# First attention's output: the few rows with an inner term computed apart, the RMS weight folded into Wo

## The chip, the cores and the metric

One program runs on one core of a Trainium2 chip. The metric is device time in microseconds: the median of three runs of the kernel before is 3495.94 (3495.18 to 3498.05). The program is a whole decoder of four layers (self attention, cross attention and a feed-forward part in each); the change touches only the last stage of the first self attention, some 63 us of it.

## The reference

The first self attention of the decoder works on B = 2 batches of 1024 tokens, 4 heads of 64, in chunks of 64 tokens. After the chunks' `W` and `U` are made, a scan over the chunks carries a state `S`; only its diagonal `Sd` is used for the output:

```python
def chunk_step(S, inp):
    q_i, k_i, w_i, u0 = inp
    Sd = jnp.diagonal(S, axis1=-2, axis2=-1)
    u_i = u0 - w_i * Sd[:, None]
    o_inter = q_i * Sd[:, None]
    A_i = jnp.tril(jnp.einsum('bchd,bchd->bc', q_i, k_i))
    o_intra = A_i[:, :, None, None] * u_i
    S = S + jnp.einsum('bchd,bche->bhde', k_i, u_i)
    return (S, o_inter + o_intra)
...
o = o * jax.lax.rsqrt(jnp.mean(o * o, axis=-1, keepdims=True) + EPS) * g
out = o.reshape(Bx, Lx, NH * HD) @ Wo
```

`A_i` is a table of batches by rows of the chunk, [2, 64], and `tril` keeps of it only row 0 of batch 0 and rows 0 and 1 of batch 1. So the inner term `A_i * u_i` is zero except in the first one or two rows of each chunk; everywhere else the output is `q_i * Sd`. `g` has one weight per place in a head (64 of them) and is the same for every head and token.

## The kernel before

The 2048 tokens lie in `NT` = 16 tiles of 128 tokens, and each tile holds two chunks of 64 (partitions 0 to 63 and 64 to 127). `QK` (trace name `q_k_tokens`) holds q and k of a token side by side, `KV` (`beta_k_v`) holds w and u by then. Work is written out in phases; inside a phase each engine has its own list of instructions and waits on semaphores, and at the end of a phase all engines meet. There is no planner: the order is the order of the code.

Three phases matter here. In the **scan phase** VectorE scans the chunk sums into `diag`, the diagonal of the state before each of the 32 chunks (32 x 256), while GpSimd builds `sel`, a 32 x 2048 table that is 1 where a token belongs to a chunk, and `rowm`, the mask of first rows. Then comes `arrive`, in which SyncE waits until all late loads have landed. Then the **output phase**:

- TensorE (L3197) multiplies `sel` by `diag` for each tile: this spreads the chunk's diagonal over its 128 tokens, into one of four PSUM banks. One such float32 product is two MATMUL records in the trace.
- VectorE does for each tile (L3213 to L3220): the dot product of q and k, w times d, the dot times the mask, u minus that, q times d, and dot times u plus q times d into `O`. There are three drains per tile, each of which lets the pipeline run empty.
- ScalarE squares each tile of `O` (L3244) into one of two buffers, VectorE sums per head (L3224), and when all 16 are summed one square root (L3246) and one reciprocal (L3226) follow.
- VectorE multiplies each tile by the reciprocal (L3230), GpSimd multiplies it by `g` (L3236), TensorE turns it (L3203, two transposes), and ScalarE copies it to `OT` (L3249).

Last, `finish` multiplies by `Wo` (L162), adds the residual and does the layer norm; its own order is not touched.

## Time and profile before

| what | us |
|---|---|
| median of three runs | 3495.94 |
| profiled execution, its own time | 3497.36 |
| span of its trace | 3495.6 |
| scan phase begins | 243.6 |
| output phase, first product to last copy | 248.75 to 311.64 |
| of this: products (16 tiles on VectorE) | 250.0 to 287.7 |
| of this: squares and sums | 287.8 to 295.3 |
| of this: scaling, weight, turning and copying | 296.3 to 311.6 |
| next phase (`finish`) begins | 311.9 |

Times within the trace count from its start. Busy time of an engine is read beside its idle time: an engine that is nearly always busy in a stretch sets its length. "Granted clock" is TensorE's, as a share of 2.4 GHz, so 0.50 is the 1.2 GHz level.

### The profile page before, as it was taken

What the parts mean: (1) busy time and instruction counts of PE and PEld (TensorE: products, weight loads), DVE (VectorE), ACT (ScalarE), POOL (GpSimd) and SP (SyncE); (2) the same over time, 40 slices, a digit from 0 to 9 for tenths busy, and PEclk for the clock granted to TensorE, in tenths of its full rate; (3) what the DMA queues carried; (4) which work ended last, traced back from release to release, by engine and by line L of the source; (5) the groups of instructions that cost most, each with busy time, mean ns of one, the idle gap of its engine ahead of it and who ended that gap; (6) DMA issues with size and microseconds to landing.
All of it is one profiled execution on the core that took longest, in us unless ns stands there. A gap on an engine that the chain in (4) does not pass through costs nothing. (4 is left out here: it accounts for less than half of the span.)

```text
span 3495.6 us, 54010 instructions
## 1 busy us (share of the span) xinstructions
PE 2866.3 (82%) x18533; PEld 1739.5 (50%) x18565; DVE 1939.8 (55%) x4670; ACT 1564.7 (45%) x4333; POOL 712.8 (20%) x790
## 2 busy tenths in 40 slices
PE   6586994845999998679968998989988968959993
PEld 3443562332555555345634653446533445639993
DVE  6546674343878876576726662156522647842333
ACT  4313782322777776572224562135521228813331
POOL 3201010021211220012104560045500102301113
PEclk9686996868999999889978999999999989959996
DMA  1000002010000000000001001000000000051112
GB/s 68 1 2 14 1 2 79 0 55 12 1 1 2 1 2 24 37 13 1 17 0 38 1 1 59 0 6 1 1 27 12 7 21 2 2 223 32 36 36 80
DMA packets 34789, 80.46 MB, mean 23 GB/s; under 512 B 8577, under 2 KB 23570, under 8 KB 30450
## 3 DMA queue, kind: packets, MB, share of 16 engines
q1 hardware_dynamic: 29746, 64.61, 5.1%
q0 software_dynamic: 4368, 11.93, 1.2%
q8 instruction: 137, 2.24, 0.3%
q14 instruction: 106, 0.87, 0.1%
q10 hardware_dynamic: 432, 0.80, 0.1%
HBM read 63.31 MB, written 14.02 MB: 22 GB/s over the span
## 5 line engine op out<-in xcount | busy, mean ns | idle before, releaser
L2436 ACT ACTIVATE scores<-scores,min 128x128 f32<-128x128 f32 (+7 forms) x256 | 198.5, 775 | 86.1 <-DVE min L2419 82.1
L2417 DVE TENSOR_SCALAR zero_marks<-psum 128x128 f32<-128x128 f32 (+7 forms) x256 | 192.0, 750 | 66.6 <-PE psum L2349 64.8
L2419 DVE CUSTOM_DVE_ANT_0 scores<-psum,zero_marks 128x128 f32<-128x128 f32 (+7 forms) x256 | 193.9, 758 | 29.9 <-issue 0.9
L2356 PE MATMUL psum<-ident,scores 128*128 128x128 f32 x1152 | 172.8, 277 | 16.4 <-ACT probsT L2453 13.3
L2453 ACT ACTIVATE probsT<-psum 128x128 f32<-128x128 f32 (+7 forms) x256 | 163.0, 637 | 31.7 <-PE psum L2356 31.1
L3684 PE MATMUL psum<-Hn,W 128*128 128x512 f32 x384 | 170.1, 606 | 8.2 <-PEq L415 8.2
L1574 ACT ACTIVATE XT<-psum,b_of_tile 128x128 f32<-128x128 f32 x312 | 89.0, 368 | 177.5 <-PE psum L1494 177.5
L1494 PE MATMUL psum<-x_gatheredT,XT 128*128 128x128 f32 x1248 | 152.0, 281 | 6.0 <-issue 3.1
L1494 PEld LDWEIGHTS psum<-x_gatheredT,XT 128*128 128x128 f32 x1248 | 147.1, 196 | 12.9 <-issue 11.8
L2356 PEld LDWEIGHTS psum<-ident,scores 128*128 128x128 f32 x1152 | 123.2, 141 | 55.8 <-issue 29.8
L2346 PE MATMUL psum<-XT,Q_heads 64*128 64x512 f32 x256 | 143.7, 641 | 0.0
L3542 POOL TENSOR_TENSOR probs<-probs,stat 128x512 f32<-128x512 f32 (+1 forms) x128 | 123.2, 986 | 99.8 <-DVE stat L3506 97.3
L1503 PE MATMUL psum<-W,XT 128*128 x624 | 141.2, 379 | 0.6 <-DVE y L1548 0.6
L3556 ACT ACTIVATE probs<-psum,stat 128x256 f32<-128x256 f32 (+1 forms) x256 | 114.4, 460 | 47.1 <-DVE stat L3499 47.1
L3410 POOL TENSOR_TENSOR straight<-straight,crossed 128x512 f32<-128x512 f32 x64 | 81.1, 1268 | 224.6 <-DVE crossed L3400 224.6
L3684 PEld LDWEIGHTS psum<-Hn,W 128*128 128x128 f32 x384 | 74.7, 195 | 103.7 <-issue 103.7
L1503 PEld LDWEIGHTS psum<-W,XT 128*128 128x128 f32 x624 | 115.5, 190 | 15.1 <-issue 1.0
L3700 DVE SCALAR_TENSOR_TENSOR GT<-psum,b,gelu 128x512 f32<-128x512 f32 x48 | 36.0, 751 | 142.0 <-ACT gelu L3694 142.0
L3499 DVE TENSOR_REDUCE stat<-psum 128x2 f32<-128x512 f32 (+1 forms) x128 | 78.1, 652 | 50.7 <-PE psum L3450 22.2
L848 ACT ACTIVATE probs<-probs,stat 128x154 f32<-128x154 f32 x256 | 104.9, 412 | 2.7 <-DVE stat L786 2.7
L2347 PE MATMUL psum<-XT,Q_heads_turned 64*128 64x128 f32 (+3 forms) x256 | 102.8, 482 | 0.0
L2340 PE MATMUL psum<-XT,Q_heads 128*128 128x128 f32 (+3 forms) x256 | 96.2, 458 | 3.3 <-POOL Q_heads L2318 2.8
(619 smaller groups left out, 6860.8 us busy)
## 6 DMA issues: line engine op xcount, KB each, us to landing
W<-in_L3f_W SPq DMA_DIRECT2D x16, 1024.0 KB, 22.5
L3f_y_rows<-y SPq DMA_DIRECT2D x39, 128.0 KB, 1.7
L0f_rows<-Xtok SPq DMA_DIRECT2D x2, 2048.0 KB, 7.7
W<-in_L0f_W SPq DMA_DIRECT2D x3, 1152.0 KB
early_weights<-in_L2f_Wqkv SPq DMA_DIRECT2D x2, 1536.0 KB
W<-in_L2f_W SPq DMA_DIRECT2D x2, 1536.0 KB
XT<-in_xT SPq DMA_DIRECT2D x1, 2048.0 KB, 10.3
Xtok<-in_xtok SPq DMA_DIRECT2D x1, 2048.0 KB
```

What stands on the lines that cost most here:

```text
L848: last = act.activation(p, src, ACT.Exp, bias=st(n, 0)[:, h:h + 1], scale=-1.0, accum_out=st(n, 1)[:, h:h + 1])
L1494: ins = pe.matmul(K.bank[2 * q + part][:, m * P:(m + 1) * P], W1t[:, k * INTER + (part * HALF + m) * P:k * INTER + (part * HALF + m + 1) * P],
L1503: ins = pe.matmul(K.bank[6][:, 0:D], HT[:, q, c, :], W2[:, bass.ds(at + c * D, D)], start=(c == 0), stop=(c == IC - 1))
L2346: pe.matmul(sc(i)[:, 0:BLK], Qh[own, u % 2, h, :], KT[own, c, b * S:b * S + BLK], start=True, stop=True, skip_group_check=True)
L2356: ins = pe.transpose(turned[:, kt * P:(kt + 1) * P], Sc[:, i % ROT, kt * P:(kt + 1) * P], K.ident[:])
L2417: dve.tensor_scalar(zero[:, i % 2, 0:n], sc(i)[:, 0:n], 0.0, -NEG, ALU.is_equal, ALU.mult)
L2419: dve.tensor_tensor_reduce(Sc[:, i % ROT, 0:n], sc(i)[:, 0:n], zero[:, i % 2, 0:n], 1.0, -NEG, ALU.add, ALU.min, low[:, i % ROT:i % ROT + ...
L2436: act.activation(p, p, ACT.Exp, bias=low[:, i % ROT:i % ROT + 1], scale=-1.0, accum_out=sums[:, u % 2, h:h + 1]).then_inc(s["exp_done"], 1)
L2453: act.activation(PT[:, i % SLOTS, 0:n], turned[:, 0:n], ACT.Copy).then_inc(s["pt_out"], 1)
L3542: pool.tensor_tensor(v, v, inner(stat[:, t % 2, 2, 2 * g:2 * g + 2], ks.stop - ks.start), ALU.mult).then_inc(s["normed"], 1)
L3556: act.activation(Pr[:, t % 2, h, ks], K.bank[2 * G + hh][:, c0 + ks.start:c0 + ks.stop], ACT.Exp, bias=stat[:, t % 2, 0, h:h + 1], scale=- ...
L3684: ins = pe.matmul(K.bank[2 * (n % 4) + part][:], W1[:, k, (part * HC + m) * P:(part * HC + m + 1) * P], Hn[:, k, j * BLK:(j + 1) * BLK], s ...
```

## The change

The output phase no longer makes the inner term for all tokens. Its parts:

- In the scan phase eight transfers between places of SBUF (four issued by SyncE for q and k, four by ScalarE for w and u) gather rows 0 and 1 of every chunk into compact tiles of 64 partitions: partition 32 i + c holds row i of chunk c. GpSimd makes `rowc`, a column of ones with zeros for row 1 of batch 0, in place of `rowm`.
- TensorE makes the diagonal for the compact rows first, in two products with 32 result rows each.
- VectorE makes the whole six-step computation once on these 64 rows, with its semaphore waits in place of drains; for each of the 16 tiles it then makes only q times d.
- SyncE writes the compact result back over rows 0 and 1 of the chunks in `O`: four transfers after the products of batch 0, four after those of batch 1. ScalarE's squares of each batch wait for them.
- Squares, sums, root, reciprocal, scaling and turning go in four groups of four tiles, with one group's squares ahead of the last group's scaling. There are four buffers of squares (two before) and two PSUM banks for the turned tiles (four before).
- `g` is loaded as one column of 128 and multiplied into `Wo` by one ScalarE instruction at the start of the phase; GpSimd has no work left in the output phase.

```diff
@@ -2795,7 +2795,7 @@
...
 Wo = sbuf(es, nc, "Wo", [P, DC, D])
 OT = sbuf(es, nc, "OT", [P, DC, TOK])
-g4 = sbuf(es, nc, "g", [P, D])
+gc = sbuf(es, nc, "g", [P, 1])
...
@@ -2819,7 +2819,7 @@
             @block.sync
             def _(sp):
-                sp.dma_start(g4[:], spread(w["L0a_g"])).then_inc(K.late, 16)
+                sp.dma_start(gc[:], w["L0a_g"][0:P].rearrange("(p o) -> p o", o=1)).then_inc(K.late, 16)
                 sp.dma_start(Wo[:], w["L0a_Wo"]).then_inc(K.late, 16)
             @block.gpsimd
@@ -3145,8 +3145,26 @@
     diag = sbuf(q_life, nc, "diagonal", [NCH, D])
     sel = sbuf(q_life, nc, "chunk_select", [NCH, TOK])
-    rowm = sbuf(q_life, nc, "first_rows", [P, B])
+    CR = 2 * P // CH * NT
+    C4 = 2 * NT
+    rowc = sbuf(q_life, nc, "row_within_batch", [CR, 1])
+    qk_c, wu_c = (sbuf(q_life, nc, n, [CR, 2 * D]) for n in ("first_rows_q_k", "first_rows_w_u"))
+    PER = NT // B
+    first_rows = lambda v, i, half, t: v[half * CH + i:half * CH + i + 1, t, :]
+    of_rows = lambda v, i, half, t: v[i * C4 + 2 * t.start + half:i * C4 + 2 * t.stop:2, :]
+    rows_of = [(i, half) for i in range(B) for half in range(2)]
+    K.late_count += 16 * 2 * len(rows_of)
     with ExitStack() as inn, phase(nc, K.sems, "step scanned turned") as (block, s):
+        @block.sync
+        def _(sp):
+            for i, half in rows_of:
+                sp.dma_start(of_rows(qk_c, i, half, slice(0, NT)), first_rows(QK, i, half, slice(0, NT))).then_inc(K.late, 16)
+        @block.scalar
+        def _(act):
+            for i, half in rows_of:
+                act.dma_start(of_rows(wu_c, i, half, slice(0, NT)), first_rows(KV, i, half, slice(0, NT))).then_inc(K.late, 16)
...
@@ -3154,12 +3172,11 @@
         def _(pool):
             v = sel[:].rearrange("p (n j) -> p n j", j=CH)
             pool.memset(sel[:], 1.0).then_inc(s["step"], 1)
-            pool.memset(rowm[:], 1.0).then_inc(s["step"], 1)
+            pool.memset(rowc[:], 1.0).then_inc(s["step"], 1)
             pool.wait_ge(s["step"], 2)
             pool.affine_select(out=v, in_=v, compare_op=ALU.is_equal, fill=0.0, base=0, pattern=[[-1, NCH], [0, CH]], channel_multiplier=1)
-            pool.affine_select(out=rowm[0:CH], in_=rowm[0:CH], compare_op=ALU.is_ge, fill=0.0, base=0, pattern=[[1, B]], channel_multiplier=-1)
-            pool.affine_select(out=rowm[CH:P], in_=rowm[CH:P], compare_op=ALU.is_ge, fill=0.0, base=0, pattern=[[1, B]], channel_multiplier=-1)
+            pool.memset(rowc[C4:C4 + 2 * PER], 0.0)
         @block.vector
         def _(dve):
@@ -3182,71 +3199,114 @@
     arrive(nc, K)
-    with ExitStack() as inn, phase(nc, K.sems, "d_done o_done squared summed root scaled o_normed turned out") as (block, s):
-        tmp = sbuf(inn, nc, "tmp", [P, 2, D])
-        dot = sbuf(inn, nc, "dot", [P, NT])
-        sq = sbuf(inn, nc, "squares", [P, 2, D])
+    with ExitStack() as inn, phase(nc, K.sems, "d_done rows_d_done dot_done dot_cut wd_done u_done qd_done rows_done rows_in0 rows_in1 o_done squared summed root recip scaled turned out") as (block, s):
+        rows_in = (s["rows_in0"], s["rows_in1"])
+        wd, u_c, qd, o_c = (sbuf(inn, nc, n, [CR, D]) for n in ("rows_w_d", "rows_u", "rows_q_d", "rows_o"))
+        dot = sbuf(inn, nc, "dot", [CR, 1])
+        sq = sbuf(inn, nc, "squares", [P, 4, D])
         ms = sbuf(inn, nc, "mean_square", [P, NT, L0H])
         O = sbuf(inn, nc, "O", [P, NT, D])
+        GRP = 4
+        groups = [range(a, a + GRP) for a in range(0, NT, GRP)]
+        @block.sync
+        def _(sp):
+            sp.wait_ge(s["rows_done"], 1)
+            for b in range(B):
+                sp.wait_ge(s["o_done"], (b + 1) * PER)
+                own = slice(b * PER, (b + 1) * PER)
+                for i, half in rows_of:
+                    sp.dma_start(first_rows(O, i, half, own), of_rows(o_c, i, half, own)).then_inc(rows_in[b], 16)
         @block.tensor
         def _(pe):
+            cut = sel[:, 0:TOK:CH]
+            for i in range(B):
+                ins = pe.matmul(K.bank[6][i * C4:(i + 1) * C4, 0:D], cut, diag[:], start=True, stop=True, skip_group_check=True)
+            ins.then_inc(s["rows_d_done"], 1)
             for t in range(NT):
                 if t >= 4:
                     pe.wait_ge(s["o_done"], t - 3)
                 pe.matmul(K.bank[t % 4][:, 0:D], sel[:, t * P:(t + 1) * P], diag[:], start=True, stop=True).then_inc(s["d_done"], 1)
             for t in range(NT):
-                pe.wait_ge(s["o_normed"], t + 1)
-                if t >= 4:
-                    pe.wait_ge(s["out"], t - 3)
+                pe.wait_ge(s["scaled"], t + 1)
+                if t >= 2:
+                    pe.wait_ge(s["out"], t - 1)
                 for c in range(DC):
-                    ins = pe.transpose(K.bank[4 + t % 4][:, c * P:(c + 1) * P], O[:, t, c * P:(c + 1) * P], K.ident[:])
+                    ins = pe.transpose(K.bank[4 + t % 2][:, c * P:(c + 1) * P], O[:, t, c * P:(c + 1) * P], K.ident[:])
                 ins.then_inc(s["turned"], 1)
         @block.vector
         def _(dve):
-            for t in range(NT):
-                q_, k_ = QK[:, t, 0:D], QK[:, t, D:2 * D]
-                a, b_ = tmp[:, 0, :], tmp[:, 1, :]
+            def product(t):
                 dve.wait_ge(s["d_done"], t + 1)
-                d_ = K.bank[t % 4][:, 0:D]
-                dve.tensor_tensor_reduce(a, q_, k_, 1.0, 0.0, ALU.mult, ALU.add, dot[:, t:t + 1])
-                dve.tensor_tensor(b_, KV[:, t, 0:D], d_, ALU.mult)
-                dve.drain()
-                dve.tensor_tensor(dot[:, t:t + 1], dot[:, t:t + 1], rowm[:, t // 8:t // 8 + 1], ALU.mult)
-                dve.tensor_tensor(b_, KV[:, t, D:2 * D], b_, ALU.subtract)
-                dve.tensor_tensor(a, q_, d_, ALU.mult)
-                dve.drain()
-                dve.scalar_tensor_tensor(out=O[:, t, :], in0=b_, scalar=dot[:, t:t + 1], in1=a, op0=ALU.mult, op1=ALU.add).then_inc(s["o_done"], 1)
-                dve.drain()
-            for t in range(NT):
-                dve.wait_ge(s["squared"], t + 1)
-                dve.reduce_sum(ms[:, t, :], sq[:, t % 2, :].rearrange("p (h d) -> p h d", h=L0H), AX).then_inc(s["summed"], 1)
-            dve.wait_ge(s["root"], 1)
-            dve.reciprocal(ms[:], ms[:])
-            dve.drain()
-            for t in range(NT):
-                v = O[:, t, :].rearrange("p (h d) -> p h d", h=L0H)
-                dve.tensor_tensor(v, v, inner(ms[:, t, :], D // L0H), ALU.mult).then_inc(s["scaled"], 1)
-        @block.gpsimd
-        def _(pool):
-            for t in range(NT):
-                pool.wait_ge(s["scaled"], t + 1)
-                pool.tensor_tensor(O[:, t, :], O[:, t, :], g4[:], ALU.mult).then_inc(s["o_normed"], 1)
+                dve.tensor_tensor(O[:, t, :], QK[:, t, 0:D], K.bank[t % 4][:, 0:D], ALU.mult).then_inc(s["o_done"], 1)
+            def sums_of(g):
+                for t in groups[g]:
+                    dve.wait_ge(s["squared"], t + 1)
+                    dve.reduce_sum(ms[:, t, :], sq[:, t % 4, :].rearrange("p (h d) -> p h d", h=L0H), AX).then_inc(s["summed"], 1)
+            def scale(g):
+                a = groups[g]
+                dve.wait_ge(s["root"], g + 1)
+                dve.reciprocal(ms[:, a.start:a.stop, :], ms[:, a.start:a.stop, :]).then_inc(s["recip"], 1)
+                dve.wait_ge(s["recip"], g + 1)
+                for t in a:
+                    v = O[:, t, :].rearrange("p (h d) -> p h d", h=L0H)
+                    dve.tensor_tensor(v, v, inner(ms[:, t, :], D // L0H), ALU.mult).then_inc(s["scaled"], 1)
+            d_c = K.bank[6][0:CR, 0:D]
+            dve.tensor_tensor_reduce(u_c[:], qk_c[:, 0:D], qk_c[:, D:2 * D], 1.0, 0.0, ALU.mult, ALU.add, dot[:]).then_inc(s["dot_done"], 1)
+            dve.wait_ge(s["rows_d_done"], 1)
+            dve.tensor_tensor(wd[:], wu_c[:, 0:D], d_c, ALU.mult).then_inc(s["wd_done"], 1)
+            dve.tensor_tensor(qd[:], qk_c[:, 0:D], d_c, ALU.mult).then_inc(s["qd_done"], 1)
+            dve.wait_ge(s["dot_done"], 1)
+            dve.tensor_tensor(dot[:], dot[:], rowc[:], ALU.mult).then_inc(s["dot_cut"], 1)
+            dve.wait_ge(s["wd_done"], 1)
+            dve.tensor_tensor(u_c[:], wu_c[:, D:2 * D], wd[:], ALU.subtract).then_inc(s["u_done"], 1)
+            product(0)
+            dve.wait_ge(s["dot_cut"], 1)
+            dve.wait_ge(s["qd_done"], 1)
+            dve.wait_ge(s["u_done"], 1)
+            dve.scalar_tensor_tensor(out=o_c[:], in0=u_c[:], scalar=dot[:], in1=qd[:], op0=ALU.mult, op1=ALU.add).then_inc(s["rows_done"], 1)
+            for t in range(1, NT):
+                product(t)
+            sums_of(0)
+            for g in range(len(groups)):
+                if g + 1 < len(groups):
+                    sums_of(g + 1)
+                scale(g)
         @block.scalar
         def _(act):
-            for t in range(NT):
-                act.wait_ge(s["o_done"], t + 1)
-                if t >= 2:
-                    act.wait_ge(s["summed"], t - 1)
-                act.activation(sq[:, t % 2, :], O[:, t, :], ACT.Square).then_inc(s["squared"], 1)
-            act.wait_ge(s["summed"], NT)
-            act.activation(ms[:], ms[:], ACT.Sqrt, scale=1.0 / (D // L0H), bias=K.eps[:, 0:1]).then_inc(s["root"], 1)
-            for t in range(NT):
-                act.wait_ge(s["turned"], t + 1)
-                act.activation(OT[:, :, t * P:(t + 1) * P], K.bank[4 + t % 4][:, 0:D].rearrange("p (c k) -> p c k", c=2), ACT.Copy).then_inc(s["out"], 1)
+            def squares(g):
+                for t in groups[g]:
+                    if t % PER == 0:
+                        act.wait_ge(rows_in[t // PER], 16 * len(rows_of))
+                    if t >= 4:
+                        act.wait_ge(s["summed"], t - 3)
+                    act.activation(sq[:, t % 4, :], O[:, t, :], ACT.Square).then_inc(s["squared"], 1)
+            def root(g):
+                a = groups[g]
+                act.wait_ge(s["summed"], a.stop)
+                act.activation(ms[:, a.start:a.stop, :], ms[:, a.start:a.stop, :], ACT.Sqrt, scale=1.0 / (D // L0H), bias=K.eps[:, 0:1]).then_inc(s["root"], 1)
+            def turned_out(g):
+                for t in groups[g]:
+                    act.wait_ge(s["turned"], t + 1)
+                    act.activation(OT[:, :, t * P:(t + 1) * P], K.bank[4 + t % 2][:, 0:D].rearrange("p (c k) -> p c k", c=2), ACT.Copy).then_inc(s["out"], 1)
+            act.activation(Wo[:].rearrange("p c n -> p (c n)"), Wo[:].rearrange("p c n -> p (c n)"), ACT.Copy, scale=gc[:, 0:1])
+            squares(0)
+            for g in range(len(groups)):
+                if g + 1 < len(groups):
+                    squares(g + 1)
+                root(g)
+                if g >= 1:
+                    turned_out(g - 1)
+            turned_out(len(groups) - 1)
 finish(nc, K, lambda k, t: Wo[:, k, :], tile_of_block(OT), DC)```

On VectorE, in the output phase, before the change (`tmp` and `first_rows` are scratch and mask; this piece comes 16 times, then 16 sums and 16 scalings):

```order
L3213 ISA tmp,dot<-q_k_tokens 128x256
L3213 ISA dot 128x1
L3214 TENSOR_TENSOR tmp<-beta_k_v,psum 128x256
L3216 TENSOR_TENSOR dot<-dot,first_rows 128x1
L3217 TENSOR_TENSOR tmp<-beta_k_v,tmp 128x256
L3218 TENSOR_TENSOR tmp<-q_k_tokens,psum 128x256
L3220 SCALAR_TENSOR_TENSOR O<-tmp,dot 128x256
```

And what stands there on VectorE after the change (`rows_...` are the compact tiles):

```order
L3265 TENSOR_TENSOR dot<-dot,row_within_batch 64x1
L3267 TENSOR_TENSOR rows_u<-first_rows_w_u,rows_w_d 64x256
L3243 TENSOR_TENSOR O<-q_k_tokens,psum 128x256
L3272 SCALAR_TENSOR_TENSOR rows_o<-rows_u,dot,rows_q_d 64x256
L3243 TENSOR_TENSOR O<-q_k_tokens,psum 128x256 x15
L3248 TENSOR_REDUCE mean_square<-squares 128x4 x8
L3253 RECIPROCAL mean_square<-mean_square 128x16
L3257 TENSOR_TENSOR O<-O,mean_square 128x256 x4
```

One instruction per tile is left of seven, and sums and scalings now alternate in groups of four.

On ScalarE, in the scan and output phases, the difference (`Wo<-Wo,g` is the folded weight):

```order
-L3238 UNCONDITIONAL_BRANCH
-L3244 ACTIVATE squares<-O 128x256 x16
-L3246 ACTIVATE mean_square<-mean_square,eps 128x64
-L3249 ACTIVATE OT<-psum 128x2x128 x16
+L3166 DMA first_rows_w_u<-beta_k_v 16x1x512 x4
+L3301 ACTIVATE Wo<-Wo,g 128x512
+L3289 ACTIVATE squares<-O 128x256 x8
+L3294 ACTIVATE mean_square<-mean_square,eps 128x16
+L3289 ACTIVATE squares<-O 128x256 x4
+L3294 ACTIVATE mean_square<-mean_square,eps 128x16
+L3299 ACTIVATE OT<-psum 128x2x128 x4
```

The copies of a group now stand behind the squares of the group after the next, in one queue on ScalarE.

## Rows read from the trace of the kernel before

**Rows 1.** Windows: length; busy PE, PEld, DVE, ACT, POOL (starts); clock; transfers' share, GB/s.
```profile
260.00:270.00 10.00, 5.43 (x10) 1.98 (x8) 8.80 (x31) 0.00 (x0) 0.00 (x0) 0.50 0.00 0
300.00:308.00 8.00, 6.36 (x19) 2.61 (x18) 8.00 (x10) 3.47 (x10) 8.00 (x10) 0.50 0.00 0
```

**Rows 2.** Timeline, scan phase's GpSimd work: start, length, engine, line, [idle <- releaser].
```profile
243.63 1.79 POOL L3156 MEMSET chunk_select<- 32x2048 f32 x1 [34.05 <-POOLq L54]
247.89 0.18 POOL L3162 TENSOR_SCALAR_AFFINE_SELECT first_rows<-first_rows 64x2 f32<-64x2 f32 x1
248.75 3.05 PEld L3197 LDWEIGHTS psum<-diagonal,chunk_select 32*128 32x128 f32 x8 [3.10 <-issue]
```

**Rows 3.** Timeline, one tile's products on VectorE, and the last one.
```profile
250.00 0.42 DVE L3213 CUSTOM_DVE_ANT_0 tmp<-q_k_tokens 128x256 f32<-128x256 f32 x1 [3.62 <-PE psum L3197]
...
256.01 0.41 DVE L3218 TENSOR_TENSOR tmp<-q_k_tokens,psum 128x256 f32<-128x256 f32 x1
...
257.11 0.43 DVE L3213 CUSTOM_DVE_ANT_0 tmp<-q_k_tokens 128x256 f32<-128x256 f32 x1
...
287.25 0.48 DVE L3220 SCALAR_TENSOR_TENSOR O<-tmp,dot 128x256 f32<-128x256 f32 x1
```

**Rows 4.** Timeline, from the squares to the start of the next phase.
```profile
289.75 0.75 DVE L3224 TENSOR_REDUCE mean_square<-squares 128x4 f32<-128x256 f32 x2 [0.22 <-ACT squares L3244]
295.34 0.35 ACT L3246 ACTIVATE mean_square<-mean_square,eps 128x64 f32<-128x64 f32 x1 [0.49 <-DVE mean_square L3224]
296.34 12.87 DVE L3230 TENSOR_TENSOR O<-O,mean_square 128x256 f32<-128x256 f32 x16
309.86 1.37 PE L3203 MATMUL psum<-ident,O 128*128 128x128 f32 x4 [0.18 <-POOL O L3236]
311.26 0.38 ACT L3249 ACTIVATE OT<-psum 128x256 f32<-128x256 f32 x1 [0.30 <-PE psum L3203]
311.93 7.31 PEld L162 LDWEIGHTS psum<-Wo,OT 128*128 128x128 f32 x28 [1.10 <-issue]
```

**Rows 5.** Timeline of an earlier phase, and L3230's row (durations min/median/max).
```profile
127.27 11.89 POOL L2970 TENSOR_TENSOR q_k_tokens<-q_k_tokens,norms 128x256 f32<-128x256 f32 x16 [4.36 <-DVEq L2953]
127.28 12.15 DVE L2957 TENSOR_TENSOR q_k_tokens<-q_k_tokens,norms 128x256 f32<-128x256 f32 x16
139.52 5.45 DVE L2960 TENSOR_TENSOR beta_k_v<-q_k_tokens,beta 128x256 f32<-128x256 f32 x16
L3230 DVE TENSOR_TENSOR O<-O,mean_square x16: 418/943/944, 296.3 to 308.3; 128x256 f32<-128x256 f32 x16
```

**Rows 6.** TensorE: lines' rows (durations, starts), windows, and one timeline row.
```profile
L3197 PE MATMUL psum<-diagonal,chunk_select x8: 626/626/759, 248.8 to 251.9; 32*128 32x256 f32 x8
L162 PE MATMUL psum<-Wo,OT x18: 379/379/379, 315.2 to 318.8; 128*128 128x256 f32 x18
...
253.00:254.00 1.00, 0.52 (x2) 0.50 0.00 0
...
336.39 9.94 PE L374 MATMUL psum<-XT,early_weights 128*128 128x512 f32 x16 [1.10 <-PEq L415]
...
314.00:315.00 1.00, 1.00 (x5) 0.79 (x4) 0.42 (x1) 0.00 (x0) 0.00 (x0) 0.60 1.10 336
...
342.00:343.00 1.00, 1.00 (x3) 0.95 0.00 0
```

**Rows 7.** An issue on SyncE's queue; issues with KB each and us to landing.
```profile
312.29 0.43 SPq L154 DMA_DIRECT2D early_weights<-in_L0x_Wk  x1
...
L3f_y_rows<-y SPq DMA_DIRECT2D x39, 128.0 KB, 1.7
L0f_rows<-acc SPq DMA_DIRECT2D x1, 512.0 KB, 2.8
Wd<-in_L1a_Wd SPq DMA_DIRECT2D x1, 128.0 KB, 2.0
b<-in_L3f_b SPq DMA_DIRECT2D x1, 32.0 KB, 25.1
```

## The prediction

> **What bounds the kernel now.** I read the windows of the output phase first, then its timeline, then the rows of single lines. In the windows VectorE is busy 8.80 of 10 us while it makes the products, TensorE works half the time at clock 0.50, and GpSimd does nothing; in the scaling, VectorE and GpSimd are both busy 8.00 of 8 us [rows 1]. The timeline gives the same in time. VectorE starts the first tile at 250.00 and the fourth at 257.11, so one tile takes (257.11 - 250.00) / 3 = 2.37 us, and the last ends at 287.25 + 0.48 = 287.73 [rows 3]. ScalarE squares the first two tiles early and then waits for VectorE, so 14 of 16 squares lie in the stretch behind the products, 287.8 to 295.3, at about 0.48 us a tile. The root starts at 295.34, the scaling of 16 tiles takes 12.87 us from 296.34, and turning and copying follow it with the last copy ending at 311.26 + 0.38 = 311.64; the next phase starts its weights at 311.93 [rows 4]. No other phase runs beside this one, since all engines meet at its ends. Whatever the output phase and the entry to it lose, the kernel loses, one for one.
>
> **The entry.** GpSimd sets the end of the scan phase: its work begins at 243.63 and ends at 247.89 + 0.18 = 248.07, and TensorE's first weights load at 248.75 [rows 2]. The change takes away two small mask steps (0.18 each by the row) and adds one memset shorter than either, so GpSimd ends near 247.8. In its place comes a new wait: four transfers on SyncE's queue and four on ScalarE's, at 0.43 us each to issue plus a gap to 0.47 (rows 7 has the 0.43), so the last is issued at 243.63 + 3 x 0.47 = 245.0. The trace shows no transfer from SBUF to SBUF. The nearest rows are 1.7, 2.0 and 2.8 us from issue to landing for 128, 128 and 512 KB; the rows moved here are 32 KB a transfer [rows 7]. With 2.0 they land at 247.0, before GpSimd ends; with 2.8 at 247.8, level with it. I take the start of the phase as unchanged, 248.75, with -0.3 and +1.0 as bounds.
>
> **The products.** TensorE has two more products than before, 18 in place of 16, each of two passes: 36 passes. At clock 0.50 eight passes start from 248.8 to 251.9, 0.44 us apart, and one lasts 0.63 [rows 6]. VectorE's one instruction per tile costs 0.41 (L3218, the same instruction) [rows 3], less than TensorE's 0.88 per tile, so TensorE becomes the pace: 35 x 0.44 = 15.4, to 264.15, plus 0.63 plus 0.41 gives **265.2** for the end of the products, against 287.73: 22.5 us less. The compact computation (two products for it first on TensorE, counted above; seven instructions on VectorE, each no longer than 0.48, 2.4 us in all with hand-overs of about 0.1 added to some) is hidden: it starts when the compact diagonal is there, near 250.8, delays tile 0's product to about 252.5, and TensorE first needs a bank back for tile 4 at 248.75 + 12 x 0.44 = 254.0. Without that cover it would cost its 2.4 us. The two compact products write different partitions; if they run beside each other the sum is 0.9 lower.
>
> **The rows written back.** SyncE's first four transfers are issued when tile 7 is done, eight tiles or 7 us ahead of the end of the products, and have landed by 265.2 - 7.0 + 3 x 0.47 + 2.0 = 261.6: hidden. The four for batch 1 start at 265.2 and land at 265.2 + 0.1 + 1.4 + 2.0 = **268.7**. Queued behind this wait on ScalarE are the squares of groups 2 and 3, the roots 1 to 3, and every copy to `OT`. VectorE is not idle meanwhile: it sums groups 0 and 1 (8 tiles at 0.36, from 0.75 for two [rows 4]) until 268.2 and scales group 0 from 268.5.
>
> **The scaling.** In place of 12.87 us for 16 tiles [rows 4] I take 5.45. The evidence is in this trace: 16 multiplies of 128x256 by a spread-out column take 12.15 us beside GpSimd's own 11.89 us of the same work, and the 16 that follow with GpSimd idle take 5.45; and L3230 itself has a minimum of 418 ns against a median of 943, its first instance starting before GpSimd has anything to do [rows 5]. GpSimd's weight step is gone, so four tiles cost 1.4.
>
> The Trainium skill (SBUF — State Buffer, section SBUF: two separate sides) says that VectorE, with two inputs from SBUF, and GpSimd hold a port pair exclusively, one blocking the other for a whole instruction. The trace agrees, by 5.45 against 12.15 us; the rule would give the same sum.
>
> **The tail.** From 268.7 ScalarE's queue is the pace, since VectorE's share for two groups of sums and three of scaling is 2 x 1.5 + 3 x 1.4 plus reciprocals, under 9. ScalarE: squares of group 2 1.4 (two take 0.75, [rows 4] by their sums), root 0.3, four copies, squares of group 3 1.4, root 0.3, four copies, root 0.3, eight copies. A copy is 0.38, and four transposes take 1.37 [rows 4]; with two banks one bank's round is 0.69 + 0.38 + 0.1 of hand-over = 1.17 for two tiles, which makes about 2.0 for a group whose first two tiles wait already. Sum: 2 x 1.4 + 3 x 0.3 + 4 x 2.0 = 11.7, so the last copy ends at **280.4**. The weight's fold costs one ScalarE instruction of 128x512 at the start of the phase, when ScalarE waits for the first rows until 261.6: hidden. Its price uncovered would be under 0.8, twice a 128x256 copy.
>
> **The sum.** 311.64 - 280.4 = 31.2 us less. Of it 22.5 are the products, 7.4 the faster scaling, and the rest the overlap less the 3.5 us wait for rows. Against the profiled execution's 3497.36 that is 3466.2; the median lies 1.4 below that execution, which gives **3465**. Bounds: entry -0.3 to +1.0, compact products 0 to -0.9, landings 1.7 to 2.8 in place of 2.0, -0.3 to +0.8, copies at 0.38 a tile as floor (-1.9 in all, as the first groups are covered) or 0.69 (+2.8): 3462 to 3470 with the clock at 0.50.
>
> **The rivals.**
>
> The clock rises in the products. Before, TensorE worked half the time there and never left 0.50; now it has no pause until its last tile. For it: with the products of `finish`, begun at 311.96, the clock has risen within 314 to 315, and with those begun at 336.39 just after 342, so 2.9 and 5.6 us on [rows 4, 6]. Against it: the first products here already ran without a pause from 248.75, ten starts up to 253, and at 254 the clock is still 0.50 [rows 6]; they hold 32 partitions, the others 128. If it rises at about 4.7 us, 11 passes are done and 25 go at (318.8 - 315.2) / 17 = 0.21 [rows 6], 0.42 a tile, level with VectorE's 0.41: 25 x 0.23 = 5.7 less. That gives 3459.5.
>
> The Trainium skill (TensorE: Matmul & The Clock Gate, Part 1) has the throttle released by sustained matmul activity; by it alone this rival would be the forecast. The trace agrees at 314.8 and 342 and does not at 253 to 254.
>
> The scaling stays slow, so that the change doesn't do what it says: then the 943 ns come from writing in place, not from GpSimd. For it: L2957 writes to the tile it reads and L2960 does not. Against it: L3230's first instance is in place and takes 418 [rows 5]. VectorE would be the pace: 12.87 / 16 = 0.80 a tile, scale 0 from 268.5 to 271.7, then three times sums 1.5, 0.2 and scaling 3.2, the last turned and copied 1.2 on: 287.6 at most, 285 to 286 with overlaps of successive instructions. That is 5.5 more: 3470.5.
>
> Landings are slow for single-partition transfers, say 5 us: the entry is 245.0 + 5.0 + 0.7 = 250.7, 2.0 later, and the rows come 3.0 later: 3470.
>
> Slower than before: each transfer lands like the slowest small one in the trace, `b<-in_L3f_b`, 32 KB, 25.1 us [rows 7]. Then the entry moves by 245.0 + 25.1 + 0.7 - 248.75 = 22.1 and the last squares by 23.1, in all 45.2 on 3465: 3510. It decides from about 18 us a landing. Against it: that transfer was one of a row of large loads from HBM, and here nothing else moves: the transfers' share in this stretch is 0.00 [rows 1].
>
> **Chances.** Forecast 0.52, clock rising 0.27, slow landings 0.09, slow scaling 0.07, slower 0.03, something that eats the gain whole 0.02. The likeliest gives 3465. The range reaches down past 3459.5 with the same spread below, 3457, and up over both 3470s with half of theirs, 3474. Faster than before by over 0.2% (7 us, about what a measurement of this kernel can tell from no change): 0.95; within: 0.02; slower: 0.03.
>
> **What would show it.** In the profile after: the first products' weights still at 248 to 249; TensorE without a pause for some 15 us at clock 0.50, and L3243 16 times at about 0.41; L3219's rows landing some 2 us after issue and ScalarE's first square of group 2 waiting for them; L3257 at 415 ns, not 830 or 943; the next phase's first weights at 280 to 281. Wrong would be: a clock of 1.00 within the products (gain near 36), the squares of group 2 waiting over 5 us, L3257 over 800 ns, or `finish` or a later phase longer than before by a microsecond or more.

## The result and the profile after

The changed kernel takes 3467.9 us (median of five runs, 3465.74 to 3476.39) where the kernel before takes 3495.18 beside it (five runs, 3490.76 to 3498.05). The ratio is 0.9929, with a 95% interval of 0.9917 to 0.9942: faster by about 0.7%. The forecast was 3465, in a range of 3457 to 3474.

Times of the trace count from its start, and the scan phase itself begins 1.14 us earlier than before (242.49 against 243.63 [rows 2]). The code ahead of it differs only in how `g` is loaded, and in the twelve kernels below the scan phase begins anywhere from 241.09 to 243.78, so nothing is read from this. Stages are therefore compared from the start of the scan phase, GpSimd's first memset of `chunk_select`. This is the timeline of after: start, length, engine, line, output and input; in brackets the idle time ahead of the group and what ended it.

```profile
242.48 2.94 SPq L3161 DMA_DIRECT2D first_rows_q_k<-q_k_tokens  x4
242.49 1.79 POOL L3174 MEMSET chunk_select<- 32x2048 f32 x1 [34.06 <-POOLq L54]
242.50 2.93 ACTq L3166 DMA_DIRECT2D first_rows_w_u<-beta_k_v  x4
246.59 0.09 POOL L3179 MEMSET row_within_batch<- 16x1 f32 x1
250.15 1.08 PE L3225 MATMUL psum<-diagonal,chunk_select 32*32 32x256 f32 x4 [5.36 <-PEq L415]
251.16 14.02 PE L3230 MATMUL psum<-diagonal,chunk_select 32*128 32x256 f32 x32
265.22 0.42 DVE L3243 TENSOR_TENSOR O<-q_k_tokens,psum 128x256 f32<-128x256 f32 x1 [0.43 <-PE psum L3230]
268.45 1.43 DVE L3257 TENSOR_TENSOR O<-O,mean_square 128x256 f32<-128x256 f32 x4
269.66 1.33 ACT L3289 ACTIVATE squares<-O 128x256 f32<-128x256 f32 x4 [2.06 <-DMA O<-rows_o]
279.31 0.81 ACT L3299 ACTIVATE OT<-psum 128x256 f32<-128x256 f32 x2 [0.42 <-PE psum L3236]
280.54 0.81 ACT L3299 ACTIVATE OT<-psum 128x256 f32<-128x256 f32 x2 [0.42 <-PE psum L3236]
281.63 8.12 PEld L162 LDWEIGHTS psum<-Wo,OT 128*128 128x128 f32 x28 [1.10 <-issue]
```

To be seen are four things. GpSimd is done at 246.7, yet the first product waits until 250.15. Then 36 passes follow without a pause. The last product of VectorE ends at 265.22 + 0.42 = 265.64, and ScalarE's squares of the second batch begin only at 269.66, released by a transfer. From there ScalarE works through its queue, with a pause of 0.42 at each of the last pairs of copies. Against [rows 4] the scaling of four tiles takes 1.43, not a quarter of 12.87 = 3.22.

These are single lines of after: issues and the scaling (shortest, median and longest in ns, then the first and the last start).

```profile
L3161 SPq DMA_DIRECT2D first_rows_q_k<-q_k_tokens x4: 609/684/823, 242.5 to 244.7; - x4
L3219 SPq DMA_DIRECT2D O<-rows_o x8: 634/634/770, 258.9 to 267.7; - x8
L3257 DVE TENSOR_TENSOR O<-O,mean_square x16: 415/418/425, 268.4 to 278.0; 128x256 f32<-128x256 f32 x16
```

And windows of after: stretch, length, busy time, then the granted clock, the share of the transfers and GB/s. The first is of all engines (PE, PEld, DVE, ACT, POOL), the second of TensorE alone.

```profile
244.00:246.00 2.00, 0.40 (x2) 0.11 (x2) 0.75 (x2) 0.00 (x0) 1.93 (x3) 0.80 0.97 47
...
254.00:258.00 4.00, 4.00 (x11) 0.50 0.00 0
262.00:265.00 3.00, 3.00 (x8) 0.50 0.01 3
```

TensorE is busy 4.00 of 4 us and still at clock 0.50, the 1.2 GHz level. The gathering transfers fill 0.97 of the queues' time and move 47 GB/s.

| step (us) | before | forecast | after |
|---|---|---|---|
| scan phase's start to first product | 5.15 | 5.12 | 7.66 |
| first product to end of VectorE's last | 38.95 | 16.45 | 15.49 |
| from there to the first square of tile 8 | | 3.5 | 4.02 |
| from there to the last copy's end | | 11.7 | 11.69 |
| start of scan to start of `finish` | 68.30 | 37.1 | 39.14 |

The forecast counted from the first load of weights, 0.03 ahead of the first product [rows 2].

The two phases are 68.30 - 39.14 = 29.2 us shorter; 31.2 were forecast. The whole trace is 27.8 shorter (3495.6 and 3467.8): the scan phase starts 1.14 earlier, `finish` takes 25.76 to the next phase's first product where it took 24.47 (+1.29), and all that comes later adds the other 1.2.

### The profile page after: what moved, and what is told of

Same layout as the page of the kernel before. It is cut to its first block and busy times, and to the rows that moved or that the text cites. A ratio compares the mean times of both kernels' runs of the same rounds, so it can differ in the third digit from the quotient of the medians.

```text
span 3467.8 us, 53877 instructions
## 1 busy us (share of the span) xinstructions
PE 2858.7 (82%) x18537; PEld 1737.6 (50%) x18569; DVE 1908.2 (55%) x4584; ACT 1564.9 (45%) x4337; POOL 699.3 (20%) x773
## 3 DMA queue, kind: packets, MB, share of 16 engines
HBM read 63.18 MB, written 14.02 MB: 22 GB/s over the span
## 6 DMA issues: line engine op xcount, KB each, us to landing
L3f_y_rows<-y SPq DMA_DIRECT2D x39, 128.0 KB, 1.7
```

## The experiments

Each stage length below is read from the kernel's own trace, from its scan phase's start as above. The table stands first; all columns but the first are in us, and `its length` runs from the start of `finish` to the next phase's first product. For the four kernels with one run the total is not read. Of the other edits to the changed kernel, only three_parts and all_four have a ratio to before whose interval lies clear of after's 0.9917 to 0.9942; what fold_undone, held_128 and wait_later are worth is read from stage lengths alone.

| kernel | first product | last product's end | first square of tile 8 | last copy's end | start of `finish` | its length | median (runs) |
|---|---|---|---|---|---|---|---|
| before | 5.15 | 44.10 | | 68.02 | 68.30 | 24.47 | 3495.18 (5) |
| after | 7.66 | 23.15 | 27.17 | 38.86 | 39.14 | 25.76 | 3467.9 (5) |
| fold_alone | 5.14 | 44.10 | | 59.70 | 59.98 | 23.32 | 3483.43 (6) |
| fold_undone | 7.81 | 23.30 | 27.32 | 42.48 | 42.75 | 25.39 | 3470.76 (5) |
| held_128 | 7.66 | 18.56 | 22.58 | 34.28 | 34.56 | 26.43 | 3470.24 (4) |
| wait_later | 4.90 | 20.39 | 24.40 | 36.10 | 36.38 | 25.29 | 3465.9 (4) |
| four_banks | 7.66 | 23.15 | 27.17 | 36.72 | 37.00 | 23.64 | 3463.02 (1) |
| qk_gathered_earlier | 5.12 | 20.60 | 24.62 | 36.32 | 36.59 | 25.18 | 3470.78 (1) |
| two_queues_back | 7.67 | 23.15 | 25.93 | 37.63 | 37.90 | 26.47 | 3470.89 (1) |
| no_inner_term | 4.90 | 19.35 | 21.27 | 33.72 | 33.99 | 26.50 | 3470.08 (1) |
| three_parts | 4.93 | 16.67 | 20.68 | 31.47 | 31.74 | 25.89 | 3454.66 (4) |
| all_four | 4.88 | 16.60 | 19.36 | 30.36 | 30.64 | 23.56 | 3454.61 (4) |

**fold_alone**: the kernel before with the weight's fold and nothing else.

```diff
-pool.tensor_tensor(O[:, t, :], O[:, t, :], g4[:], ALU.mult).then_inc(s["o_normed"], 1)
+act.activation(Wo[...], Wo[...], ACT.Copy, scale=gc[:, 0:1])   # first on ScalarE
-pe.wait_ge(s["o_normed"], t + 1)
+pe.wait_ge(s["scaled"], t + 1)
```

> The kernel before with one part of the change: g is loaded as a column and multiplied into Wo by ScalarE, GpSimd does nothing in the output phase. Theory (GpSimd slows VectorE): the scaling falls from 12.87 us to about 5.5, turning and copying become the pace at about 0.43 a tile, the phase ends about 7 us earlier, 3488. Rival (writing in place makes it slow): L3230's successor stays near 0.80 a tile and only GpSimd's lag goes, about 1 us, 3494.

Measured: ratio 0.9966 (0.9954 to 0.9978); the phases are 68.30 - 59.98 = 8.3 us shorter. The scaling in its timeline:

```profile
295.51 5.46 DVE L3230 TENSOR_TENSOR O<-O,mean_square 128x256 f32<-128x256 f32 x16
```

The same instruction, writing in place, takes 5.46 in place of 12.87 [rows 4] once GpSimd no longer works beside it. The rival by which writing in place was slow is dead. The phases gained a little more than the 7 expected.

**fold_undone**: the changed kernel with GpSimd's step put back between scaling and turning, and the fold gone (the diff above, reversed).

> The changed kernel with one part undone: GpSimd multiplies each tile by g between scaling and turning, Wo is left as it is. Theory: the scaling goes back from 418 ns to 830 or 943, VectorE becomes the pace behind the rows' wait, the phase is 5 to 6 us longer, 3473. Rival (ScalarE's queue is the pace anyway): the phase is under 2 us longer.

Measured: ratio to before 0.9937 (0.9924 to 0.9951), the phases 3.6 us longer than after's. That lies between the 5 to 6 of the theory and the rival's under 2. Two rows of its timeline:

```profile
272.75 2.49 DVE L3257 TENSOR_TENSOR O<-O,mean_square 128x256 f32<-128x256 f32 x4
273.25 3.26 POOL L3285 TENSOR_TENSOR O<-O,g 128x256 f32<-128x256 f32 x4 [0.73 <-DVE O L3257]
```

Four tiles cost VectorE 2.49 beside GpSimd's 3.26, against 1.43. So the fold is worth 8.3 us in the old order and 3.6 in the new one, where part of the slow scaling lies beside ScalarE's squares and copies. With GpSimd's step left as it was, the rest of the change is worth 68.30 - 42.75 = 25.5. The Trainium skill (SBUF — State Buffer, section SBUF: two separate sides) says that whichever of the two engines starts first holds their shared port pair for its whole instruction. The traces agree that each slows the other: VectorE's instruction has a median of 942 ns beside GpSimd and takes 418 without it, GpSimd's takes 902 beside VectorE and 719 without it. They do not show that one stands still for the whole of the other, since a pair of instructions comes every 0.86 us, less than 0.42 + 0.72.

**held_128**: as after, but the products hold all 128 partitions, with zeros in the new 96 rows of the diagonal. VectorE clears those rows in the scan phase, where GpSimd also makes its last memset ahead of the mask; the entry stays 7.66.

```diff
-diag = sbuf(q_life, nc, "diagonal", [NCH, D])
-sel = sbuf(q_life, nc, "chunk_select", [NCH, TOK])
+diag = sbuf(q_life, nc, "diagonal", [P, D])
+sel = sbuf(q_life, nc, "chunk_select", [P, TOK])
...
+dve.memset(diag[NCH:2 * NCH], 0.0)
+dve.memset(diag[2 * NCH:P], 0.0)
```

> The changed kernel with the spreading products holding 128 partitions in place of 32 (chunk_select and diagonal are padded with zeros; same columns, same number of passes). Theory (the clock stays at 0.50 because these products hold 32 partitions): the clock rises within 3 to 6 us of the phase's first product, the 16 products take 9 to 10 us in place of 14.0, the phase is 4 to 5 us shorter, 3463. Rival (the number of partitions doesn't matter): clock 0.50 to the last product and no change in the phase.

Measured: ratio 0.9923 (0.9905 to 0.9941). Its TensorE, the timeline and the windows around the rise:

```profile
251.44 1.09 PE L3228 MATMUL psum<-diagonal,chunk_select 128*32 128x256 f32 x4 [5.36 <-PEq L415]
252.45 9.43 PE L3233 MATMUL psum<-diagonal,chunk_select 128*128 128x256 f32 x32
...
254.00:257.00 3.00, 3.00 (x9) 0.50 0.00 0
257.00:260.00 3.00, 3.00 (x16) 0.99 0.00 0
```

The same 36 passes in the same order: held on 32 partitions, they ran their 15 us at 0.50; held on 128, the clock rose 5.6 us after the first (257.0 - 251.44) and the products ended 4.6 earlier. All of it reached the last copy (34.28 against 38.86). But the clock fell again at 267.3, `finish` had it back only 6.0 us after its start and took 26.43, and the median, 3463 by the theory, came out at 3470.24, not distinguishable from after's. The rise comes back in three_parts and all_four, 4.4 us after their first product. The Trainium skill (TensorE: Matmul & The Clock Gate, Part 1) has sustained matmul activity release the throttle; held_128 agrees, after does not, by the windows at 254 to 265 above.

**wait_later**: the gathers count on a semaphore of their own, so the phase opens without them, and VectorE makes tiles 0 to 3 before it waits for them.

```diff
-K.late_count += 16 * 2 * len(rows_of)
...
-sp.dma_start(of_rows(qk_c, ...), first_rows(QK, ...)).then_inc(K.late, 16)
+sp.dma_start(of_rows(qk_c, ...), first_rows(QK, ...)).then_inc(gathered, 16)
...
+for t in range(4):
+    product(t)
+dve.wait_ge(gathered, 16 * 2 * len(rows_of))
```

> The changed kernel with the wait for the eight gathering transfers taken out of the meeting before the output phase and put on VectorE, behind the products of tiles 0 to 3; the compact computation follows there. Theory (the entry lost 2.5 us to the transfers, the rest of the phase does not depend on them): from the scan phase's start to the first spreading product 5.1 us in place of 7.7, the whole 2.5 us shorter, 3465. Rival (the wait only moves): VectorE waits over 1 us for the rows behind tile 3 and the phase ends within 0.5 us of the changed kernel's.

Measured: ratio 0.9918 (0.9903 to 0.9934). TensorE, and one transfer row (KB each, median us from issue to landing):

```profile
248.40 1.08 PE L3226 MATMUL psum<-diagonal,chunk_select 32*32 32x256 f32 x4 [2.60 <-PEq L415]
...
first_rows_q_k<-q_k_tokens SPq DMA_DIRECT2D x4, 32.0 KB, 4.4
```

The first product comes 4.90 after the scan phase's start, 2.76 earlier than after's, and the gain stays whole to the last copy (38.86 - 36.10 = 2.76). So the entry's loss was the wait for the gathers and nothing else. A gather of q and k takes 4.4 us to land by the median, 3.4 to 5.0 in all, where 2.0 was taken.

**qk_gathered_earlier**: the four gathers of q and k are issued in the phase before, with the same wait as after.

```diff
-sp.dma_start(of_rows(qk_c, ...), first_rows(QK, ...)).then_inc(K.late, 16)   # in the scan phase
+sp.dma_start(of_rows(qk_c, ...), first_rows(QK, ...)).then_inc(K.late, 16)   # one phase ahead
```

> The changed kernel with the four gathering transfers of q and k issued one phase earlier (where the w and u products are made), so that only the four of w and u are left in the scan phase. Theory (the 128 packets of 2 KB were slow, up to 1.09 us each, because they all read from the same few partitions at once): the packets of each four take about half as long, the four of w and u land by about 247, GpSimd's mask sets the entry again, and scan start to first product is 5.1 to 5.6 us in place of 7.7. Rival (a fixed latency of such a transfer): packets as long as before, and the entry still over 7 us.

Measured: the first product at 5.12, as early as before the change, with half of the gathers still waited for. The windows with these four in flight:

```profile
244.00:246.00 2.00, 0.39 (x2) 0.11 (x2) 1.03 (x2) 0.00 (x0) 1.93 (x3) 0.88 0.68 48
246.00:248.00 2.00, 0.12 (x2) 0.15 (x4) 0.07 (x1) 0.14 (x1) 0.93 (x2) 0.50 0.24 17
```

With four gathers in flight the rate is 48 GB/s, with eight it was 47. The four are issued 0.63 us apart, and 32 KB every 0.63 us is 52 GB/s, so they ran near the pace of their issues. The eight came from two engines at about twice that pace and got no more: 256 KB took from 243.76 to 249.25. Packets of 2 KB took up to 0.67 us with four (0.45 in the mean) and up to 1.09 with eight (0.50), so the theory's half holds for the longest and not for the mean. Each gather reads one partition (0, 1, 64 or 65). That these few partitions are what held the eight to 47 GB/s is not shown: a gather spread over many partitions wasn't run.

**four_banks**: four PSUM banks for the turned tiles, as in the kernel before.

```diff
-if t >= 2:
-    pe.wait_ge(s["out"], t - 1)
+if t >= 4:
+    pe.wait_ge(s["out"], t - 3)
-ins = pe.transpose(K.bank[4 + t % 2][...], ...)
+ins = pe.transpose(K.bank[4 + t % 4][...], ...)
```

> The changed kernel with four PSUM banks for the turned tiles in place of two. Theory (with two banks a tile's transposes wait for the copy of the tile two before, so the last eight copies go at 0.61 us each): they go at under 0.5 us each and the phase ends 1 to 1.5 us earlier, 38.9 us after the scan phase's start becoming under 38. Rival (ScalarE's own queue of squares, roots and copies is the pace): under 0.3 us.

Measured: the last copy 2.14 us earlier, more than the 1 to 1.5 expected. ScalarE's last eight copies are one group now, where they came in pairs 1.23 us apart (279.31 and 280.54 above):

```profile
274.44 3.37 ACT L3299 ACTIVATE OT<-psum 128x256 f32<-128x256 f32 x8 [0.85 <-PE psum L3236]
```

**two_queues_back**: of the eight transfers that write rows back, GpSimd's queue issues half.

```diff
-for i, half in rows_of:
-    sp.dma_start(first_rows(O, ...), of_rows(o_c, ...)).then_inc(rows_in[b], 16)
+rows_back(sp, rows_of[0::2], rows_in)
+rows_back(pool, rows_of[1::2], rows_in_too)
```

> The changed kernel with the four write-back transfers of each batch issued by two engines, SyncE and GpSimd, two each. Theory (3 of the 4.0 us between the last product and the square of tile 8 are four issues of 0.68 us in a row): the wait falls to about 2.7 us and the phase is 1 to 1.3 us shorter. Rival (GpSimd's transfers start later than SyncE's, about 1 us by their queue): no gain, or up to 1 us longer.

Measured: from the last product's end to the square of tile 8 it takes 2.78, not 4.02, and the phases lose the same 1.24. ScalarE's row:

```profile
269.18 1.34 ACT L3297 ACTIVATE squares<-O 128x256 f32<-128x256 f32 x4 [0.82 <-DMA O<-rows_o]
```

**no_inner_term** leaves out the gathers, the compact rows and their write-back, so its rows 0 and 1 lack the inner term.

```diff
-ins = pe.matmul(K.bank[6][i * C4:(i + 1) * C4, 0:D], cut, diag[:], ...)
-dve.tensor_tensor_reduce(u_c[:], qk_c[:, 0:D], qk_c[:, D:2 * D], ...)      # and the five steps behind it
-act.wait_ge(rows_in[t // PER], 16 * len(rows_of))
+act.wait_ge(s["o_done"], t + 1)
```

> The changed kernel without the inner term: no gathering, no compact computation, no write-back, the squares wait for each product alone (the first rows' inner term is left out of the output). It shows what the few rows cost in all. Theory (2.5 us at the entry, 1.0 for TensorE's two compact products, and about 3 of the 4.0 before the squares of tile 8, since squares that run beside the products shorten the tail too): scan and output phases 31 to 33 us in place of 39.1. Rival (VectorE's sums, scaling and ScalarE's queue behind the products are the pace, not the rows' return): 35 us or more.

Measured: the phases take 33.99 us, 5.15 less than after's, so the gain is smaller than the theory's 31 to 33 would have it. The entry gives 2.76 and the compact products 1.04 (15.49 to 14.45). The wait falls by 2.1 (4.02 to 1.92), but the tail behind it is 0.76 longer (12.45). VectorE begins its sums only behind its last product, and ScalarE's squares of tiles 4 to 7 wait for them; the first copies then wait 0.57 us at 265.42 for tiles that VectorE has scaled late, while after's, at 271.10, find them ready:

```profile
261.83 1.39 ACT L3250 ACTIVATE squares<-O 128x256 f32<-128x256 f32 x4 [10.22 <-DVE mean_square L3224]
```

This is what the inner term costs now: 5.15 of 39.14 us.

**three_parts** is wait_later, held_128 and four_banks together; **all_four** has the two queues for the write-back as well. Their edits are the diffs above.

> The changed kernel with three edits together: the wait for the gathered rows behind tile 3's product, the spreading products holding 128 partitions, and four PSUM banks for the turned tiles. If the single gains add (2.8 and 4.6 us measured, 1 to 1.5 expected), the scan and output phases take 30 to 31 us in place of 39.1 and the whole about 8 us less than the changed kernel, 3460. Rival (the clock then falls or the rows come back too late): the compact rows are not ready for the write-back of batch 0, or the wait before the squares of tile 8 grows, and the gain is under 6 us.

> The three edits together (31.7 us for the two phases) and the write-back split over SyncE and GpSimd, which alone took 1.24 us off. Theory: 30.5 us, the whole about 1 us below the three edits, 3453 to 3454; against the changed kernel about 14 us less. Rival (the wait is covered by something else by now): two phases within 0.3 us of 31.7.

Measured: three_parts has a ratio of 0.9887 (0.987 to 0.9903), all_four 0.9886 (0.9869 to 0.9902). Singly the three parts gave 2.76 + 4.58 + 2.14 = 9.5 us, together 39.14 - 31.74 = 7.4. The timelines show the two places where the other 2.1 went. The first, in all_four, is the same in three_parts:

```profile
253.96 3.72 PE L3241 MATMUL psum<-diagonal,chunk_select 128*128 128x256 f32 x16 [1.15 <-DVE O L3254]
```

With the faster clock TensorE runs out of banks while VectorE is in the compact computation: 1.15 us of idle time, where after has none. wait_later, with the same order at clock 0.50, has none either, so the cover that the forecast named for this computation is lost where the clock has risen by then. From the first product to VectorE's last, three_parts takes 11.74 us and held_128 10.90, 0.84 less.

The second place, in three_parts, is behind the products, which end at 258.57:

```profile
259.58 2.56 ACT L3295 ACTIVATE squares<-O 128x256 f32<-128x256 f32 x8 [12.05 <-DMA O<-rows_o]
260.02 2.70 DVE L3252 TENSOR_REDUCE mean_square<-squares 128x4 f32<-128x256 f32 x8 [1.46 <-ACT squares L3295]
```

The rows of batch 0 now come back behind the last product, where in after they were home by 263.05, ahead of its end at 265.64. So the squares of tiles 0 to 7 and VectorE's sums start a microsecond late, and the tail behind the first square of tile 8 takes 10.79 us against 9.55 in four_banks, the other 1.24. The rival on record with three_parts looked near here: it had the compact rows not ready for this write-back. They were ready, SyncE issues it at 255.41, but from there to the first square it takes 4.2 us, which the shorter products no longer cover.

all_four is 1.1 us shorter than three_parts in the phases and 2.3 in `finish`, yet equal in the median (3454.61 and 3454.66), so this difference lies below what the totals tell. Both beat the changed kernel, by 13.2 and 13.3 us in the median.

## Why the prediction was right, and the step that was mis-sized

- **Direction and size: right.** The phases lost 29.2 us of the 31.2 forecast, and the products gave most of it, as said. The scaling's share is smaller than the 7.4 named for it: with everything else in place it is worth 3.6 (fold_undone).
- **The entry: mis-sized.** "I take the start of the phase as unchanged, 248.75, with -0.3 and +1.0 as bounds" failed: it came 2.5 later (7.66 against 5.15), outside the bounds. Two inputs were wrong. A gather's issue took 0.61 to 0.82 us on SyncE, not the 0.43 of [rows 7], so the last stood 2.2 us behind the scan's start and not 1.4. And it landed 4.4 us after issue by the median and 5.0 at most (read in wait_later), not 2.0. The slow-landings rival had priced about that at the entry (5 us a landing, 2.0 later), but put the same delay on the rows written back, and those did not have it. wait_later and qk_gathered_earlier each took the delay away alone.
- **The products: right.** TensorE was the pace at clock 0.50, 0.44 a pass (32 passes in 14.02), VectorE waited 0.43 for each tile. They took 15.49, not 16.45: the two compact products ran beside each other, four passes in 1.08 us, which was the -0.9 given as a bound.
- **The clock rival: did not happen here**, though it did in held_128, at 5.6 us. The stated evidence against it, 32 partitions held and not 128, is the one difference between the two kernels' products. Had it risen as in held_128, the phases would have lost 4.6 more, not the 5.7 that the rival named.
- **The compact computation: hidden, as said**, at this clock. At the higher one, where it stands behind tile 3, it is not (1.15 us of idle time in all_four).
- **The rows written back: right to 0.5.** They landed 2.0 us after the last issue (267.7 to 269.66), as taken; the issues stood 0.68 apart in place of 0.47, and 3 x 0.21 = 0.6 makes the difference of 4.02 and 3.5.
- **The scaling: right.** 418 ns against 415 forecast; fold_alone has 5.46 for 16 tiles, where 5.45 was forecast.
- **The slow-scaling rival: priced too high**, 5.5 against the 3.6 of fold_undone. It took 3.2 for each group of four tiles; a group takes 2.49 in the row above, because its first two instructions run at 418 to 426 ns before GpSimd has a tile.
- **The tail: right**, 11.69 against 11.7. The round of the two banks was in the sum at 1.17 for two tiles and measured 1.23; with four banks the tail is 2.14 shorter, where the bound said 1.9.
- **`finish` and the rest: not in the sum.** The prediction named a microsecond more there as a sign of being wrong, and `finish` took 1.29 more: that sign did show. The 2.5 us of `finish` and later phases, less the 1.14 ahead of the scan, are the difference between 29.2 and 27.8. That the scan phase began earlier is luck: no term of the sum has it.

What stays open is how far the later drift is the clock's; `finish` below shows the pattern, the phases behind it weren't told apart.

## What to carry to other kernels

When a step is replaced by many small transfers that one wait collects, price them as a queue: time between issues (0.6 to 0.8 us here), and one rate for all that are in flight together (47 GB/s for eight here). Let the wait stand where their result is first used, not at the door of the phase. Where a cheap multiply on a second engine touches the same tiles, ask first what it costs the first engine: here it doubled each instruction (418 to 943 ns), and a constant factor was folded into the next weights by one instruction of 0.72 us, while ScalarE waited anyway. When one stage's pace changes, the covers named for the others must be worked out anew: with the products 4 us shorter, both the compact computation and the first write-back came into the open.

## What the runs showed of the hardware

- **A phase's length went with when the clock rose in it.** `finish` runs the same code in all twelve kernels and took 23.3 to 26.5 us. With the clock at 1.00 when it began it took 23.32 (fold_alone, up since 2.6 us), 23.56 (all_four, 0.9) and 23.64 (four_banks, 0.4); with a rise 2.9 us after its start (before) 24.47, 3.7 (qk_gathered_earlier) 25.18, 4.1 (wait_later) 25.29, 4.3 (fold_undone) 25.39, 4.5 (after) 25.76, about 5 (three_parts) 25.89, about 6 (held_128, two_queues_back, no_inner_term) 26.4 to 26.5. The later the rise, the longer the phase, but for 0.04 us among the last three. So a gain of 1 to 4 us ahead of it can be lost in it, as in held_128, and single totals (after's own run from 3465.74 to 3476.39) can't tell such edits apart, while stage lengths can. For after the rise shows in this window:

```profile
286.00:287.00 1.00, 1.00 (x6) 0.84 (x5) 0.92 (x5) 0.00 (x0) 0.00 (x0) 0.93 0.94 259
```

- **Partitions held and the clock.** 15 us of products without a pause on 32 partitions left the granted clock at 0.50; the same on 128, with zeros in 96 of them, had it at 1.00 after 5.6 us (4.4 in three_parts and all_four).
- **Packets of transfers within SBUF.** Reading 32 KB from one partition to 16, the 2 KB packets took up to 1.09 us with eight such transfers in flight; writing 8 KB back to one partition, the 1 KB packets took 44 to 79 ns.
- **Two products with 32 result rows each**, the same rows held and different result partitions, overlapped almost wholly. They started in twos, at 250.15 and 250.16, then at 250.56 and 250.61: four passes in 1.08 us, while four passes of the full ones start 0.43 to 0.44 apart and take 4 x 0.44 = 1.76.
